# A GNN kernel on one core: the clear behind each indirect transfer goes, and each transfer waits for GpSimd's report on the one ahead

## The reference, cut to what matters

```python
edge_index = jnp.stack([src, dst])
h = jnp.maximum(_layernorm(x, axis=-1), 0.0)
x = x + _L0_gnn_ref(h, edge_weight, edge_attr_3, edge_index, ...)
h = jnp.maximum(_layernorm(x, axis=-1), 0.0)
x = x + _L1_gnn_ref(h, edge_index, ...)

# _L0_gnn_ref (layer 0 here)
src, dst = (edge_index[0], edge_index[1])
R = jax.nn.relu(abs_distances[:, None] @ w1 + b1) @ w2 + b2
Fj = features[src]
...
out = out.at[dst].add(msg)

# _L1_gnn_ref: three times (layers 1, 2, 3 here)
h = x @ W
msg = h[src] * norm[:, None]
out = jax.ops.segment_sum(msg, dst, num_segments=n_nodes)
```

## Time and profile before

| | |
|---|---|
| median of 3 runs | 5770.3 us (5766.36 to 5771.24) |
| span of the profiled execution | 5779.7 us |
| GpSimd busy | 4889.1 us (85%) |
| TensorE busy | 4258.6 us (74%) |
| VectorE busy | 3608.0 us (62%) |
| ScalarE busy | 2702.7 us (47%) |
| indirect transfers | 3616, busy 3636.6 us of GpSimd |
| clears of `pause` | 3616, busy 1234.8 us of GpSimd |

### The profile page before, as it was taken

One profiled execution on the slowest core, in us unless ns is written; L12 is line 12 of the kernel. 1 busy time (PEld: TensorE's weight loads), 2 busy tenths in 40 slices (PEclk: granted clock), 3 DMA queues, 4 the chain that ended last, 5 costly groups with the idle time before them and its releaser, 6 DMA issues.

```text
span 5779.7 us, 179150 instructions
## 1 busy us (share of the span) xinstructions
PE 4258.6 (74%) x62463; PEld 3147.7 (54%) x62464; DVE 3608.0 (62%) x8469; ACT 2702.7 (47%) x6550; POOL 4889.1 (85%) x7276
## 2 busy tenths in 40 slices
PE   5777777777777777755555555889898889766666
PEld 3444444444444444444444444778787778554554
DVE  8777777777777777776666666333333334555555
ACT  4444444444444444466666666344444444433333
POOL 7888888888888888768888888688888889588886
PEclk9999999999999999955555555899989999767767
DMA  3111111111111111333332332332333333444444
GB/s 87 33 33 33 33 33 31 33 33 33 33 33 32 32 33 33 36 71 77 77 77 77 77 77 71 114 90 85 91 91 85 91 91 100 119 119 126 122 127 107
DMA packets 494970, 400.88 MB, mean 69 GB/s; under 512 B 269575, under 2 KB 454828, under 8 KB 493537
## 3 DMA queue, kind: packets, MB, share of 16 engines
q10 hardware_dynamic: 146996, 207.67, 10.6%
q0 software_dynamic: 115712, 109.02, 10.3%
q1 hardware_dynamic: 231536, 74.48, 5.9%
HBM read 375.52 MB, written 15.29 MB: 68 GB/s over the span
## 4 chain that ended last, share of the span: by engine, by line
POOL 50%; issue 40%; PE 5%; POOLq 2%; DVE 2%; DMA 1%; ACT 0%; DVEq 0%; SPq 0%
POOL rows L782 29%; POOL pause L762 21%; POOLq L761 2%; PE radial L2067 2%; PE psX L2082 1%; PE psT L2082 1%; PE sums L2153 1%; PE radial L2209 0%; DMA table<-arena 0%; PE radial L2222 0%; DMA rows<-table,idx 0%; DMA xn<-in_x 0%; POOLq L760 0%; PE radial L2008 0%; DVE rows L1827 0%
## 5 line engine op out<-in xcount | busy, mean ns | idle before, releaser
L782 POOL DMA_INDIRECT rows<-table,idx x3616 | 3636.6, 1006 | 803.0 <-POOL pause L762 483.7
L762 POOL MEMSET pause<- 128x256 f32 x3616 | 1234.8, 341 | 2.5
L1942 PEld LDWEIGHTS sums<-scratch,onehot 128*64 128x64 f32 x9408 | 789.7, 144 | 465.0 <-DVE scratch L1377 228.6
L2067 PE MATMUL radial<-arena,shared 128*32 128x96 bf16 (+1 forms) x31200 | 926.4, 266 | 154.2 <-DVE shared L1613 75.1
L1942 PE MATMUL sums<-scratch,onehot 128*64 128x264 f32 (+1 forms) x9408 | 984.1, 356 | 32.6 <-DVE scratch L1377 26.2
L2067 PEld LDWEIGHTS radial<-arena,shared 128*32 128x32 bf16 (+1 forms) x31200 | 664.8, 116 | 294.4 <-issue 72.0
L2153 PE MATMUL sums<-onehot,rows 128*128 128x80 f32 (+1 forms) x2844 | 371.0, 298 | 576.7 <-DMA rows<-table,idx 571.8
L1007 ACT CAST scratch<-radial 128x480 bf16<-128x480 f32 x860 | 476.9, 555 | 665.7 <-PE radial L2067 657.6
L1360 DVE TENSOR_TENSOR scratch<-radial,shared 128x768 f32<-128x768 f32 x784 | 743.4, 948 | 0.0
L1927 PE MATMUL radial<-shared 64*128 64x384 f32 x3136 | 730.5, 546 | 0.0
L880 ACT COPY shared<-rows 128x192 f32<-128x192 f32 x196 | 89.4, 456 | 1264.1 <-DMA rows<-table,idx 1262.9
(11 more groups left out here) (237 smaller groups left out, 5969.3 us busy)
## 6 DMA issues: line engine op xcount, KB each, us to landing
scratch<-places_d ACTq DMA_DIRECT2D x242, 800.0 KB
rows<-table,idx POOLq DMA_INDIRECT x3616
shared<-in_edge_weight SPq DMA_DIRECT2D x390, 128.0 KB, 2.9
idx<-in_src SPq DMA_DIRECT2D x451, 4.0 KB
table<-arena SPq DMA_DIRECT2D x24, 256.0 KB, 2.8
table<-arena SPq DMA_DIRECT2D x2, 1176.0 KB, 10.6
accT<-in_edge_attr SPq DMA_DIRECT2D x2, 1152.0 KB
table<-arena SPq DMA_DIRECT2D x24, 96.0 KB, 2.0
```

The source lines that it names most:

```text
L762: nc.gpsimd.memset(pause[:, :], 0.0).then_inc(made, 1)
L782: (pool.indirect_dma_start(rows_3[:, r, j, :] if n in (1, 3) else rows[:, r, j, 0:WIDTH[n]], None, tables[n], bass.IndirectOffsetOnAxis(ap ...
L1942: last = nc.tensor.matmul(there, onehot[:, u % 2, 4 * h + t, 0:SW], taken_from, start=(h + q + part == 0), stop=(h == 1 and q == 1 and par ...
L2067: last = nc.tensor.matmul(d, from_src[n][:, h, i, t, :], table_of(n, s), start=True, stop=True, tile_position=(0, 32 * i))
```

## The change

The clear goes, with its tile. In its place each transfer waits on `made` until all transfers ahead of it have been reported, and the transfer itself names `made` as its `engine_sem`: GpSimd adds 1 to it when its own work on the transfer is done, with the descriptors written and the transfer started, which is not yet when the rows have landed. The count starts and goes on as before, so one transfer at a time is at work on GpSimd.

```diff
-            pauses = pool.alloc_register("pauses")
-
-            def pause_between(step, n, u, j):
+            issues = pool.alloc_register("issues")
+
+            def after_previous(step, n, u, j):
 
                 if step.peeled:
                     before = TPG * (sum(GATHERED[:n]) + step.it * step.groups + u) + j
                     if before:
                         pool.wait_ge(made, 9 + before)
                 else:
-                    pool.wait_ge(made, pool.snap(pauses))
-                    pool.reg_add(pauses, pauses, 1)
-                nc.gpsimd.memset(pause[:, :], 0.0).then_inc(made, 1)
+                    pool.wait_ge(made, pool.snap(issues))
+                    pool.reg_add(issues, issues, 1)
...
                         for j in range(TPG):
                             col = j % 2 * KS + j // 2
+                            after_previous(step, n, u, j)
                             (pool.indirect_dma_start(rows_3[:, r, j, :] if n in (1, 3) else rows[:, r, j, 0:WIDTH[n]], None, tables[n],
-                                                     bass.IndirectOffsetOnAxis(ap=idx[:, r, col:col + 1], axis=0))
-                                 .then_inc(gathered[r], 16))
-                            pause_between(step, n, u, j)
+                                                     bass.IndirectOffsetOnAxis(ap=idx[:, r, col:col + 1], axis=0),
+                                                     engine_sem=made).then_inc(gathered[r], 16))
```

More of the change, by code:

```diff
@@ L61 @@
 PAD_REL = -1000.0
-PAUSE = 256
 assert NG % UNROLL == 0 and PTAIL * KS == ETAIL and PTAIL <= P and NG == 2 * NB
@@ L295, in gnn_kernel @@
         one = sb("one", [P, 1])
-        pause = sb("pause", [P, PAUSE])
         flag = sb("flag", [P, 1])
@@ L806, in gathers @@
                     pool.reg_mov(turn[u], 2 * (LOOP[n][0] // UNROLL - 1) if n else 0)
-                pool.reg_mov(pauses, 9 + TPG * (sum(GATHERED[:n]) + LOOP[n][0]))
+                pool.reg_mov(issues, 9 + TPG * (sum(GATHERED[:n]) + LOOP[n][0]))
                 sweep(pool, body, n)
```

## The result

The changed kernel takes 6434.5 us (median of 4 runs, 6432.83 to 6437.22) against 5769.2 for the kernel before on the same chip: a ratio of 1.1155, 95% interval 1.1139 to 1.117. It is slower, as forecast, but 66 us faster than the low end of the range. The profiled executions span 6432.9 and 5779.7 us, a difference of 653 us where the steps of the prediction add up to 882. (By the medians it is 665; the profiled execution of the kernel before was some 12 us longer than its others.)

The account below looks back on a forecast made before the run. GpSimd's pace per transfer was taken to bound the kernel. Loops +951, longer waits +25 and peeled parts -94 gave +882 us on 5770, about 6650 us, with a range of 6500 to 7050.

Parts of the forecast that it names:

- What bounds the kernel, and the direction: Whole kernel: for the length of a layer GpSimd's pace per transfer sets the time; slower 88%, same 3%, faster 9%.
- In a loop nothing of the next transfer's preparation lies beside the work ahead: Loops, 3040 transfers: a register instruction waits directly ahead of each transfer, so preparation is serial; +951 us.
- Its size, 0.81 us of gap: Loops: 0.03 us to the register instruction plus 0.78 to the transfer's start, replacing about 0.49 to 0.52 us.
- The excess stays where it is, on both sides: Loops: the transfers' longer mean, 1019 ns in layer 0's, comes from some longer transfers and stays unchanged; 0 us.
- the 0.95 us of an undisturbed transfer: Loops: a transfer takes 0.95 us before and after, so start to start goes from 1.44 to 1.76 us.
- In the peeled parts the transfer is prepared ahead of its own wait: Peeled parts: gap 0.28 us instead of 0.49, a gain of 0.21 for 448 transfers, -94 us.
- rival B: Peeled parts: nothing is prepared ahead of a wait there either; +1129 us in all, 6900 us; chance 22%.
- The longer wait: Loops, every 96 transfers: the sequencer's 2.35 us more all shows, where run-ahead hid all but 1.54; +25 us.
- Layer 2's close gains nothing: Last 128 peeled transfers of layer 2: no gain, since TensorE is busy 217 of 224 us there.
- Rival C: Layer 0: TensorE becomes the bound if its granted clock falls to 0.54; +265 us, 6915 us; chance 10%.
- Rival D: All 3616 transfers: the report comes later than the transfer row's end, 362 us per 0.1 us; 7010 us and more; 6%.
- the gap's 0.03 us: Loops: uncertainty of 0.03 us either way on the gap, 91 us over 3040 transfers; forecast's own range 6550 to 6750.

Follow-up runs that it names:

- clear_then_wait: The kernel before with its wait put ahead of each transfer instead of behind it, the clear kept: 7635.5 us, ratio 1.3225.
- carried: The changed kernel with each transfer in the loops too carrying its wait, on a constant, with no register read: 4988.1 us, ratio 0.8651.
- two_in_flight: The changed kernel with each transfer waiting for the one two ahead, in the loops still at the register instruction: 4979.4 us, ratio 0.8636.
- longer_clear: The kernel before with a clear of 616 columns instead of 256, nothing else changed: 6760.3 us, ratio 1.1704.
- clear_448: The kernel before with a clear of 448 columns instead of 256: 6253.0 us, ratio 1.0842.
- clear_192: The kernel before with a clear of 192 columns instead of 256: 5552.1 us, ratio 0.9623.
- small_multiply: The kernel before with VectorE's multiply of arena and rows in layer 0's loop doing one tile of a group's eight: 5680.9 us, ratio 0.9842.
- peeled_only: The change in the peeled parts alone, the loops keeping the clear behind each transfer as in the kernel before: 5702.8 us, ratio 0.9887.

## Why the prediction was wrong, step by step

- **What bounds the kernel, and the direction: right.** GpSimd's pace sets the time; slower, as given 88%.
- **In a loop nothing of the next transfer's preparation lies beside the work ahead: right.** `clear_then_wait` shows it without a report, and `carried` and `two_in_flight` take the cost away.
- **Its size, 0.81 us of gap, was too large by 0.046.** The term came from one place, where the register instruction stood right behind a turn of the loop and the transfer started 0.78 us after it. In the steady loop it is 0.73, and the gap 0.763 to 0.767. That is 0.046 x 3040 = 139 us less. The turns of the loops, which the sum left out on both sides, give 15 back: above the ordinary gap, five in layer 1 and five in layer 2 cost 35 us now and the same ten 20 us before. Together -124 of the -126 in the first row of the table.
- **"The excess stays where it is, on both sides": wrong.** This is the step that failed, and with it the 0.95 us of an undisturbed transfer, which was to stay too: 135 us together. The median transfer in the loops went from 0.953 to 0.942 us, which makes 35 of the 135. What transfers take beyond the median fell from 157 to 57 us, 100 of the 135, and 86 of these in layer 0's loop (99.5 to 13.7 us). I took this excess as a property of the transfers. In layer 0 it is a meeting with VectorE's instructions that read twice from SBUF: in its loop, 369 transfers were over 1.05 us before and 70 after. `longer_clear`, `clear_448`, `clear_192` and `small_multiply` show it for layer 0. What the excess of layers 1 to 3 comes from was not followed up. Without the 135 us the time would have been about 6570 us, inside the range; the gap's error alone would not have left it.
- **In the peeled parts the transfer is prepared ahead of its own wait: right,** with a gap of 0.30 us against 0.28; rival B is out. The Trainium skill's rule that a transfer is decoded first and then waits in a hardware queue ("Perfetto Trace Analysis", section "DMA Instruction — SWDGE (GPSIMD)") agrees with the gap of 0.30 us here, and in the loops once the transfers carry their wait. The 32 us that are missing are, by estimate, 448 x 0.02 = 9 and the groups' first transfers, whose second wait puts them in series: 55 of the 71 stand outside layer 2's close, and 55 x 0.46 = 25.
- **The longer wait: right,** 2.35 us exposed, as forecast, 31 times. **Layer 2's close gains nothing: right.** TensorE is busy 203 of 209 us at its end (below), and `peeled_only` has the same: layer 3's first transfer starts 98 us after layer 2's last has ended, 94 in the full change, 69 before.
- **Rival C, TensorE's clock: it fell, but not far enough.** The windows that answer to the earlier trace rows (busy us of PE, PEld, DVE, ACT, POOL; granted clock):

```profile
92.00:2750.00 2658.00, 1914.23 (x14055) 1165.11 (x14053) 1790.33 (x3464) 1053.26 (x3079) 1461.91 (x1536) 0.87 0.16 30
2820.90:4068.00 1247.10, 622.49 (x15341) 501.25 (x15339) 705.36 (x2383) 692.02 (x1083) 704.64 (x736) 0.55 0.27 68
5255.00:5464.00 209.00, 202.86 (x3620) 179.32 (x3619) 87.17 (x163) 98.43 (x292) 145.20 (x147) 0.97 0.35 102
```

In layer 0 the granted clock went from 0.92 to 0.87 and TensorE's busy time from 1817 to 1914 us, of 2658 now: it is not the bound. Rival D is out: the wait's row starts 0.03 us behind the transfer's end.

The range missed since its low end took in the gap's 0.03 us (91 us) and little more; it had no room for the transfers' own length.

## What to carry to other kernels

A wait on a register's value directly ahead of an indirect transfer puts the sequencer's preparation on the path, 0.46 us per transfer here; a constant that the transfer can carry, or a wait for work further back, hides it, and it is worth asking first whether the transfers need to be held apart at all. When a change shifts the pace of an engine, the part of its instructions' length that comes from meeting another engine shifts with it: look at which instructions are long, and what runs on the other engine when they start, before carrying their mean over. And a step's price that is read where other instructions stand around it is an estimate: all ten turns at which GpSimd had run dry in the kernel before show the same 0.78 us, and the steady loop of the changed kernel 0.73, 7% less.

## What the runs showed of the hardware that was not expected

- In none of the twelve traces did two indirect transfers of 128 rows start less than 1.24 us apart (0.94 and 0.30), whether they waited for each other or not.
- Behind a clear a transfer that is prepared starts after 0.16 us (0.27 where it carries a wait for that clear), behind another transfer only after 0.30.
- In layer 0's loop VectorE holds up an indirect transfer in its instructions with both operands in SBUF, and then until the instruction is over. A transfer that starts within 0.04 us of the start of VectorE's multiply is not held; the multiply is then longer instead (0.79 us, not 0.76). Elsewhere an instruction with one tile and a value per partition goes with long transfers too (52 of 76 in layer 2's loop).
- A transfer with two waits has one of them in a row of the sequencer's own, and loses 0.46 us by it.
- The longer wait at every 96th transfer, 2.35 us where a register wait exposes it, does not show at all where nothing stands between the transfers.
